# Normalised rows of a four-layer graph network: VectorE's scalar-tensor-tensor form with a repeated second tensor instead of the tensor-scalar form

## The chip, the core and the metric

The kernel runs on one core of a Trainium2 chip. The metric is the device time of one execution in microseconds (us). Three runs of the kernel before took 2252.54, 2250.71 and 2248.42 us, so the median is 2250.71 us.

## What is computed

128 boards of 64 squares, each square a row of 256 values, go through four layers. Each layer normalises its input row by row, applies relu, computes a graph network of the result and adds that to its input:

```
def _layernorm(x, axis=-1, eps=1e-05):
    m = jnp.mean(x, axis=axis, keepdims=True)
    v = jnp.var(x, axis=axis, keepdims=True)
    return (x - m) / jnp.sqrt(v + eps)

    h = jnp.maximum(_layernorm(x, axis=-1), 0.0)
    x = x + _L0_gnn_ref(h, adj, adj, ...)     # attention, 8 heads, static and adjacency masks
    h = jnp.maximum(_layernorm(x, axis=-1), 0.0)
    x = x + _L1_gnn_ref(h, adj, ...)          # attention, 4 heads, adjacency mask
    h = jnp.maximum(_layernorm(x, axis=-1), 0.0)
    x = x + _L2_gnn_ref(h, adj, ...)          # tanh of masked scores, 4 heads, gated
    h = jnp.maximum(_layernorm(x, axis=-1), 0.0)
    x = x + _L3_gnn_ref(h, adj, ...)          # as L1, other weights
```

The change touches only the line `(x - m) / sqrt(v + eps)`, as it is computed in all four layers.

## The kernel before, in words

**Tiling.** A group is 4 boards, that is 256 tokens, held as two tiles (t = 0, 1) of 128 tokens in the partitions by 256 values along the row. There are 32 groups. Two slots work on two groups at once, each with buffers of its own (X, XN, HT, SMALL, F and others carry a 0 or 1), so a loop round takes two groups through all four layers, and there are 16 rounds. Slot 1 runs about half a round behind slot 0.

**Order.** Each engine's program is a fixed list of steps in which the steps of the two slots are merged by a table (`ORDER`), and the engines meet only at semaphores. An engine works its list strictly in order, so a step that waits holds all later steps of that engine, those of the other slot too.

**One normalisation** (eight in a loop round: four layers in each of two slots; 128 in the program) goes through these steps:

- `bn`: VectorE computes statistics of tile 0 and of tile 1 of X (L931).
- `stats`: VectorE merges them into mean and variance (L938) and adds eps (L941); then GpSimd raises two values per partition to the power -0.5 (L410), which gives the reciprocal deviation RSTD, and tells VectorE.
- `norm`: VectorE writes XN = (X - mean) * RSTD, one instruction for each of the two tiles (L949), each telling TensorE when it is done. This is the step that changes.
- `turn`: TensorE transposes XN into PSUM, four 128x128 pieces: (half 0, tile 0), (half 0, tile 1), (half 1, tile 0), (half 1, tile 1) (L505). The first waits for XN's tile 0, the second for its tile 1. ScalarE applies relu and rounds to fp32r (L763), VectorE takes the remainder (L963), and TensorE multiplies both with the layer's weights (L437).

What else the text speaks of: L989, L1003, L1053, L870, L1090 and L1095 are other VectorE operations. GpSimd, beside L410, does one sum X = X + F of 128x512 values in each group's third layer (L423), and one product per group (L415, `row_terms`). On GpSimd's list, L423 of one slot follows directly behind the L410 of the other slot at the same place of every round. L714 are TensorE's transposes of F for the gate in the third layer, L848 ScalarE's copy of those (`cT`), and the `cT` rows of L870 VectorE's remainder of them.

Of the kernel before, what the change touches and what calls it, by code (L numbers as in the profile page):

```python
# [25 lines left out]
ALU = mybir.AluOpType  # L26
# [3 lines left out]
P = 128  # L30
SQ = 64
D = 256
# [107 lines left out]
def build(nc, x_in, adjq_in, adjt_in, mats_in, cols_in, rows_in, cst_in, out):  # L140
# [8 lines left out]
    with ctx:  # L149
# [3 lines left out]
        def sem(name):  # L153
            return ctx.enter_context(nc.semaphore(name))
# [18 lines left out]
        X, XN, HT, MASKA, MASKO, ADJ8, ADJT8, SMALL = ([] for _ in range(8))  # L173
# [10 lines left out]
        MV = [m[:, 12:16].rearrange("p (t c) -> p t c", t=TT) for m in SMALL]  # L184
        VE = [m[:, 16:18] for m in SMALL]
        RSTD = [m[:, 18:20] for m in SMALL]
# [57 lines left out]
        def tanh_buf(s, t):  # L244
# [10 lines left out]
        S = [{n: sem(f"{n}_{s}") for n in ONCE + TWICE + FOUR + NORM + ATTS + ["x_in", "adj_in", "adjT_in", "stored"]}  # L255
             for s in range(SLOTS)]
# [10 lines left out]
        def norm_count(a, v):  # L267

            return v.four[NORM_OF[a]]
# [596 lines left out]
        def _(dve):  # L866
            tt, ts, stt = nc.vector.tensor_tensor, nc.vector.tensor_scalar, nc.vector.scalar_tensor_tensor
# [75 lines left out]
            def norm(s, a, v, before):  # L943
                if a == 0 and before is not None:

                    dve.wait_ge(S[s]["stored"], before)
                dve.wait_ge(S[s]["rstd"], norm_count(a, v))
                for t in range(TT):
                    ts(XN[s][:, t * D:t * D + D], X[s][:, t * D:t * D + D], MV[s][:, t, 0:1],  # L949
                       RSTD[s][:, t:t + 1], ALU.subtract, ALU.mult).then_inc(S[s]["xn_ready"], 1)  # L950

            def masks(s, v):

# [12 lines left out]
            def att(s, k, a, i, v):  # L966
# [7 lines left out]
                elif k == "stats":  # L974
                    stats(s, a, v)
                elif k == "norm":
                    norm(s, a, v, v.before)
                elif k == "masks":
                    masks(s, v)
# [51 lines left out]
            def l2(s, k, i, v):  # L1031
# [3 lines left out]
                elif k == "stats":  # L1035
                    stats(s, L2, v)
                elif k == "norm":
                    norm(s, L2, v, None)
                elif k == "turn":
                    h_lo(s, i, norm_halves(L2, v))  # L1040
# [99 lines left out]
```

## Time and profile before

| | |
|---|---|
| median of three runs | 2250.71 us |
| the profiled execution, whole | 2248.06 us |
| its span, first to last instruction | 2245.9 us |
| mean granted TensorE clock | 0.967 |
| TensorE busy (matmul) | 2011.9 us, 90% |
| TensorE busy (weight loads) | 1818.6 us, 81% |
| VectorE busy | 1445.6 us, 64% |
| ScalarE busy | 1151.8 us, 51% |
| GpSimd busy | 192.2 us, 9% |

All times of single instructions come from one profiled execution. In its rows PE is TensorE's matmul, PEld its weight load, DVE is VectorE, ACT is ScalarE and POOL is GpSimd. `xn<-x,small` reads: the tile XN written from X and SMALL (SMALL holds mean, variance and RSTD). A busy share says nothing of what waits for what; the timeline and the idle times before instructions do.

### The profile page before, as it was taken

The page shows a single profiled execution, that of the slowest core. Times are in us where ns is not written, and L with a number is a line of the kernel's source. Part 1 is how long each engine was busy: PE and PEld are TensorE (multiplying, and loading weights), DVE is VectorE, ACT ScalarE, POOL GpSimd, SP SyncE. Part 2 cuts the span into 40 slices and gives each one's busy share as a digit, 9 for nine tenths or more (in the row PEclk, how much of TensorE's full clock was granted, in tenths as well). Part 3 has the DMA queues.
Part 4 walks back from the last instruction along what each step waited for, and adds up shares of the span by engine and source line. Part 5 has one row for each costly group of instructions (what it writes and reads, how often), then busy time and mean ns, then how long its engine had stood idle before and what let it go on. Part 6 is the DMA issues. An engine that isn't in the chain of part 4 may idle for free.

```text
span 2245.9 us, 53566 instructions
## 1 busy us (share of the span) xinstructions
PE 2011.9 (90%) x21228; PEld 1818.6 (81%) x21228; DVE 1445.6 (64%) x3769; ACT 1151.8 (51%) x3862; POOL 192.2 (9%) x203
## 2 busy tenths in 40 slices
PE   6699989899898989989899998989989899998997
PEld 5588878788887888878788887888888788887885
DVE  4466667667666667667666666666757666666663
ACT  3355555455455555555455454545455455455552
POOL 0000101100001100100110000100101100000100
PEclk8799999999999999999999999999999999999998
DMA  5000000000000000000000000000000000000000
GB/s 174 1 3 12 12 12 12 11 5 9 12 12 12 11 11 2 11 12 11 12 11 2 12 11 12 11 11 2 11 12 11 11 12 2 12 11 12 11 6 5
DMA packets 40630, 30.66 MB, mean 14 GB/s; under 512 B 15664, under 2 KB 40240, under 8 KB 40432
## 3 DMA queue, kind: packets, MB, share of 16 engines
q1 hardware_dynamic: 40432, 27.48, 4.1%
q8 instruction: 190, 3.11, 0.6%
q14 instruction: 8, 0.07, 0.0%
HBM read 19.08 MB, written 8.39 MB: 12 GB/s over the span
## 4 chain that ended last, share of the span: by engine, by line
PE 62%; issue 18%; DVE 12%; ACT 4%; POOL 4%; DMA 1%; DVEq 0%; SPq 0%; POOLq 0%; ACTq 0%
PE ps L437 57%; PE ps L505 4%; POOL small L410 3%; DVE small L931 2%; DVE xn L949 2%; PE ps L581 2%; ACT probs L788 1%; DVE x L1028 1%; DVE wide L1053 1%; DVE f L1062 1%; POOL x L423 1%; DVE aT L870 1%; ACT f L824 1%; ACT wide L816 1%; DVE small L938 1%
## 5 line engine op out<-in xcount | busy, mean ns | idle before, releaser
L437 PE MATMUL ps<-hT,w_hi 128*128 128x256 f32 x2560 | 511.2, 291 | 55.8 <-issue 47.7
L437 PEld LDWEIGHTS ps<-hT,w_hi 128*128 128x128 f32 x2560 | 420.5, 194 | 73.1 <-issue 50.8
L788 ACT ACTIVATE probs<-probs,small 128x64 f32<-128x64 f32 x1024 | 342.1, 339 | 33.2 <-DVE small L1009 31.4
L437 PE MATMUL ps<-hT,w_lo 128*128 128x256 f32 x1280 | 343.1, 288 | 0.0
L437 PEld LDWEIGHTS ps<-hT,w_lo 128*128 128x128 f32 x1280 | 249.2, 195 | 2.7
L437 PE MATMUL ps<-w_hi,hT 128*128 128x256 f32 (+1 forms) x1024 | 249.1, 312 | 0.0
L410 POOL TENSOR_TENSOR small<-small,consts 128x2 f32<-128x2 f32 x128 | 88.8, 694 | 1776.2 <-DVE small L941 1776.2
L437 PE MATMUL ps<-w_hi,oT 128*128 128x256 f32 x768 | 189.2, 311 | 27.4 <-DVE oT L870 27.4
L437 PE MATMUL ps<-wide,w_hi 128*128 128x256 f32 x1024 | 213.1, 285 | 0.2
L788 ACT ACTIVATION_READ_ACCUMULATOR probs<-probs,small 128x1 f32 x1024 | 196.2, 192 | 0.0
L816 ACT ACTIVATE wide<-ps,c_vec 128x256 fp32r<-128x256 f32 x256 | 107.6, 472 | 148.3 <-PE ps L437 148.3
L437 PEld LDWEIGHTS ps<-w_hi,hT 128*128 128x128 f32 x1024 | 175.4, 188 | 8.4
L1053 DVE SCALAR_TENSOR_TENSOR wide<-ps,c_vec,wide 128x256 fp32r<-128x256 f32 x256 | 109.5, 479 | 103.6 <-ACT wide L816 103.5
L437 PEld LDWEIGHTS ps<-w_hi,oT 128*128 128x128 f32 x768 | 147.5, 211 | 32.5 <-DVE oT L870 32.3
L437 PEld LDWEIGHTS ps<-wide,w_hi 128*128 128x128 f32 x1024 | 163.4, 188 | 3.1 <-DVE wide L870 0.7
L949 DVE TENSOR_SCALAR xn<-x,small 128x256 f32<-128x256 f32 x256 | 123.3, 523 | 62.0 <-POOL small L410 59.7
L437 PE MATMUL ps<-w_hi,cT 128*128 128x256 f32 x768 | 159.3, 290 | 0.3 <-ACT cT L848 0.3
L505 PE MATMUL ps<-consts,xn 128*128 128x128 f32 x512 | 116.3, 324 | 46.1 <-DVE xn L949 42.9
L437 PE MATMUL ps<-w_lo,hT 128*128 128x256 f32 (+1 forms) x512 | 149.9, 310 | 0.0
L763 ACT ACTIVATE hT<-ps 128x256 fp32r<-128x256 f32 x256 | 88.4, 383 | 98.5 <-PE ps L505 97.6
L505 PEld LDWEIGHTS ps<-consts,xn 128*128 128x128 f32 x512 | 62.5, 151 | 86.9 <-DVE xn L949 74.2
L437 PE MATMUL ps<-wide,w_lo 128*128 128x256 f32 x512 | 131.8, 280 | 0.0
(123 smaller groups left out, 4342.5 us busy)
## 6 DMA issues: line engine op xcount, KB each, us to landing
raw_mats<-mats SPq DMA_DIRECT2D x8, 1024.0 KB, 11.9
x<-x SPq DMA_DIRECT2D x32, 256.0 KB, 3.0
out<-xn SPq DMA_DIRECT2D x32, 256.0 KB, 3.0
adj<-adjq SPq DMA_DIRECT2D x64, 16.0 KB, 2.0
adjT<-adjt SPq DMA_DIRECT2D x64, 8.0 KB, 2.1
raw_consts<-board_consts SPq DMA_DIRECT2D x1, 451.5 KB, 3.1
raw_rows<-rows SPq DMA_DIRECT2D x1, 256.0 KB, 4.5
bias_cols<-cols SPq DMA_DIRECT2D x1, 6.0 KB, 3.6
```

What stands on the lines that cost most here:

```text
L410: nc.gpsimd.tensor_tensor(RSTD[s], VE[s], HALF.broadcast_to([P, TT]), ALU.pow).then_inc(sm["rstd"], 1)
L423: nc.gpsimd.tensor_tensor(X[s][:, :], X[s][:, :], F[s][:, 0:512], ALU.add).then_inc(sm["x_ha"], 1)
L437: return nc.tensor.matmul(o, lhsT, rhs, start=start, stop=stop, skip_group_check=True)
L505: last = nc.tensor.transpose(bank(s, H_BANKS[c])[:, t * P:t * P + P], XN[s][:, t * D + c * P:t * D + c * P + P], IDENT)
L581: last = nc.tensor.transpose(bank(s, 1 - i)[:, at:at + P], PR[s][:, j, at:at + P], IDENT)
L763: fn(HT[s][:, 0, c, :], bank(s, H_BANKS[c])[:, 0:TOK], ACT.Relu).then_inc(S[s]["hT_hi"], 1)
L788: last = fn(p, p, ACT.Exp, bias=ROWMAX[s][:, row:row + 1], accum_out=ROWSUM[s][:, row:row + 1])
L816: last = fn(e_view(s, 0, oc, i), e_bank(s, E_BANKS[i], oc), ACT.Identity, bias=CVEC[:, oc, i:i + 1])
L824: fn(tanh_buf(s, i), bank(s, 2 + i), ACT.Tanh).then_inc(sm["tanh"], 1)
L931: nc.vector.bn_stats(STATS[s][:, t, :], X[s][:, t * D:t * D + D]).then_inc(S[s]["bn"], 1)
L949: ts(XN[s][:, t * D:t * D + D], X[s][:, t * D:t * D + D], MV[s][:, t, 0:1], RSTD[s][:, t:t + 1], ALU.subtract, ALU.mult).then_inc(S[s]["xn ...
L1053: stt(e_view(s, 1, oc, i), e_bank(s, E_BANKS[i], oc), CVEC[:, oc, i:i + 1], e_view(s, 0, oc, i).bitcast(F32), ALU.add, ALU.subtract).then_ ...
```

## The change

The two instructions of a `norm` step are no longer the form with two per-partition scalars (`tensor_scalar`) but the fused form with a scalar and two tensors (`scalar_tensor_tensor`): (X - mean) * T, where T is the column RSTD read again for each of the 256 elements of a row, through an access pattern with step 0. Semaphores, waits, buffers, the order of all instructions and the values computed stay as they are. Later lines of the file move down by one.

```diff
@@ -946,8 +946,9 @@
                     dve.wait_ge(S[s]["stored"], before)
                 dve.wait_ge(S[s]["rstd"], norm_count(a, v))
                 for t in range(TT):
-                    ts(XN[s][:, t * D:t * D + D], X[s][:, t * D:t * D + D], MV[s][:, t, 0:1],
-                       RSTD[s][:, t:t + 1], ALU.subtract, ALU.mult).then_inc(S[s]["xn_ready"], 1)
+                    stt(XN[s][:, t * D:t * D + D], X[s][:, t * D:t * D + D], MV[s][:, t, 0:1],
+                        RSTD[s][:, t:t + 1].broadcast_to([P, D]), ALU.subtract, ALU.mult
+                        ).then_inc(S[s]["xn_ready"], 1)
```

`ts` and `stt` are `nc.vector.tensor_scalar` and `nc.vector.scalar_tensor_tensor`; D is 256, P is 128, TT is 2.

## Rows read from the trace of the kernel before

**Rows 1.** The page: busy time of each engine, and TensorE's clock in 40 slices.

```profile
PE 2011.9 (90%) x21228; PEld 1818.6 (81%) x21228; DVE 1445.6 (64%) x3769; ACT 1151.8 (51%) x3862; POOL 192.2 (9%) x203
PEclk8799999999999999999999999999999999999998
```

**Rows 2.** The page: the chain that ended last, by engine.

```profile
PE 62%; issue 18%; DVE 12%; ACT 4%; POOL 4%; DMA 1%; DVEq 0%; SPq 0%; POOLq 0%; ACTq 0%
```

**Rows 3.** Line L949 alone: durations in ns, then who waited for it (us, times).

```profile
L949 DVE TENSOR_SCALAR xn<-x,small x256: 401/410/1356, 52.4 to 2223.5; 128x256 f32<-128x256 f32 x128
...
  PEld ps L505: 74.2, 166
  PE ps L505: 42.9, 59
```

**Rows 4.** Groups of VectorE instructions: busy us, mean ns | idle before.

```profile
L1053 DVE SCALAR_TENSOR_TENSOR wide<-ps,c_vec,wide 128x256 fp32r<-128x256 f32 x256 | 109.5, 479 | 103.6 <-ACT wide L816 103.5
...
L963 DVE SCALAR_TENSOR_TENSOR hT<-ps,hT 128x256 fp32r<-128x256 f32 x256 | 99.4, 419 | 21.4 <-ACT hT L763 21.4
...
L1090 DVE SCALAR_TENSOR_TENSOR f<-xn,f 128x256 f32<-128x256 f32 x64 | 27.2, 425 | 2.2
...
L1095 DVE SCALAR_TENSOR_TENSOR x<-f,x 128x512 f32<-128x512 f32 x32 | 22.2, 693 | 3.4
...
L876 DVE TENSOR_SCALAR raw_rows<-raw_rows,raw_consts 128x1024 f32<-128x1024 f32 x1 | 0.8, 753 | 0.0
```

**Rows 5.** Timeline, a normalisation without company: start us, us, what [idle before <-releaser].

```profile
1166.67 0.69 POOL L410 TENSOR_TENSOR small<-small,consts 128x2 f32<-128x2 f32 x1 [13.26 <-DVE small L941]
...
1167.40 0.74 DVE L949 TENSOR_SCALAR xn<-x,small 128x256 f32<-128x256 f32 x2 [0.81 <-POOL small L410]
...
1167.87 1.23 PE L505 MATMUL ps<-consts,xn 128*128 128x128 f32 x4 [0.47 <-DVE xn L949]
...
1168.70 0.81 ACT L763 ACTIVATE hT<-ps 128x256 fp32r<-128x256 f32 x2 [0.82 <-PE ps L505]
```

**Rows 6.** Timeline, a normalisation that starts beside GpSimd's sum L423.

```profile
1145.24 1.28 POOL L423 TENSOR_TENSOR x<-x,f 128x512 f32<-128x512 f32 x1
1145.31 1.68 DVE L949 TENSOR_SCALAR xn<-x,small 128x256 f32<-128x256 f32 x2 [0.80 <-POOL small L410]
...
1145.48 0.60 PE L714 MATMUL ps<-consts,f 128*128 128x128 f32 x4
...
1146.72 0.87 PE L505 MATMUL ps<-consts,xn 128*128 128x128 f32 x4 [0.64 <-DVE xn L949]
1146.91 0.74 DVE L870 TENSOR_TENSOR cT<-ps,cT 128x256 fp32r<-128x256 f32 x2
1147.04 0.31 PEld L505 LDWEIGHTS ps<-consts,xn 128*128 128x128 f32 x3 [0.18 <-DVE xn L949]
```

**Rows 7.** Timeline, a normalisation where TensorE comes a little late.

```profile
1219.07 0.74 DVE L949 TENSOR_SCALAR xn<-x,small 128x256 f32<-128x256 f32 x2 [0.22 <-POOL small L410]
...
1219.57 0.83 PE L505 MATMUL ps<-consts,xn 128*128 128x128 f32 x4
...
1220.66 0.39 PE L437 MATMUL ps<-hT,w_hi 128*128 128x256 f32 x1 [0.25 <-ACT hT L763]
```

**Rows 8.** Timeline, the place where TensorE in some rounds comes later still.

```profile
1111.15 0.73 DVE L949 TENSOR_SCALAR xn<-x,small 128x256 f32<-128x256 f32 x2
...
1112.22 0.46 PEld L505 LDWEIGHTS ps<-consts,xn 128*128 128x128 f32 x4
```

**Rows 9.** Timeline, GpSimd's product L415 and VectorE's L1053 beside it.

```profile
1173.54 1.92 POOL L415 TENSOR_TENSOR row_terms<-rs,consts 128x1024 fp32r<-128x1024 f32 x1 [6.18 <-DVE rs L1048]
...
1174.79 0.88 DVE L1053 SCALAR_TENSOR_TENSOR wide<-ps,c_vec,wide 128x256 fp32r<-128x256 f32 x2 [1.33 <-ACT wide L816]
```

**Rows 10.** Two loop rounds: us, busy of PE, PEld, DVE, ACT, POOL, clock, DMA.

```profile
744.00:877.10 133.10, 121.75 (x1317) 110.08 (x1316) 88.95 (x235) 70.71 (x240) 11.89 (x13) 0.99 0.04 10
...
1281.70:1418.40 136.70, 124.23 (x1317) 112.92 (x1316) 89.07 (x235) 70.81 (x240) 11.86 (x13) 0.96 0.04 10
```

## The prediction, made before the changed kernel was run

> **What bounds the kernel now.** I read the page's busy table first: TensorE is busy 90% of the span and VectorE 64% [rows 1]. The chain that ended last lies 62% on TensorE and 12% on VectorE [rows 2]. So TensorE's fixed list sets the time, and another engine counts where TensorE stands and waits for it. Next I asked for the changed line alone: 256 instructions, median 410 ns, and TensorE does wait for them, 42.9 us ahead of its matmuls and 74.2 us ahead of its weight loads; the loads overlap matmuls, so the two are not added [rows 3]. The 166 waits of loads for 128 normalisations say that TensorE is often held a second time, by the second tile. The timelines show it. With nothing else running, the pair takes 0.74 us, TensorE has been idle for 0.47 us when its first transpose starts, and its four transposes stretch over 1.23 us [rows 5]; in rows 6, at the higher clock, they take 0.87, against 0.60 us for the four of L714, which wait for nothing. Then ScalarE and TensorE's next product hang on these transposes. VectorE's two instructions are thus on the path, and the end of the second is what counts.
>
> One kind of place is different. In each round, once in each slot, the pair starts 0.07 us behind GpSimd's sum L423 and takes 1.68 us instead of 0.74 [rows 6]. The maximum in rows 3 is the first of such a pair, 1356 ns. It ends at 1145.31 + 1.36 = 1146.67, 0.15 us behind the sum's end at 1146.52: it stood still while the sum ran, and did its reading afterwards. I counted 31 such pairs in the trace (first instruction 1341 to 1356 ns); the other 97 have first instructions of 401 to about 414 ns.
>
> **The change part by part.** Nothing is moved, no wait is added; each of the 256 instructions is exchanged for one of another form. Its price is not in the trace, so I bound it. L1053 is the same form with a per-partition scalar, 256 elements, one tensor in PSUM and one in SBUF: 479 ns. L963 is the form with a constant in place of the per-partition scalar: 419. So that scalar costs 60 ns. L1090 has a constant and both tensors in SBUF: 425 [rows 4]. The new instruction has one per-partition scalar (the mean) and two SBUF tensors: 425 + 60 = 485, or 479 by the nearest row; the bottom is 425 (no cost for the scalar). Upwards nothing in the rows goes past 485 without company; a repeated column as second tensor could be dearer, but the trace has no such row in this form. I take 480.
>
> Pairs run back to back with an overlap: 0.74 us for two of 410 ns, 0.88 us for two of 479 [rows 5, 9]. So a pair alone gets 0.88 - 0.74 = 0.14 us longer (bounds: 0.03 with 425 ns, 0.15 with 485).
>
> For a pair beside the sum I need the part that comes after the sum's end, the reading of 256 elements. Two-tensor form: 693 ns at 512 elements less 425 at 256 is 268 ns per 256. One-tensor form: 753 ns at 1024 elements (one scalar), 410 at 256 (two scalars): (753 + 60 - 410) / 768 = 0.52 ns an element, 134 ns per 256; without the correction for the scalar 114 [rows 3, 4]. So the first of the pair ends 268 - 134 = 0.13 us later (0.15 by the other figure), and the second comes 0.07 us later again, 480 less 410: 0.20 us, if it still waits for the sum. The pair would take 1.88 us.
>
> What of it is hidden? At six of the eight normalisations of a round TensorE is idle for the pair already, so all of the 0.14 or 0.20 us falls on the path. At two (one in each slot, [rows 7]) it arrives 0.09 us behind the first tile, 1219.57 against 1219.48, yet its four transposes take 0.83 us, because the second tile ends only at 1219.81; the next product then waits 0.25 us for ScalarE. The second tile's 0.14 us is on the path there too. At one of the six, in 6 of the 16 rounds, TensorE comes 0.34 us behind the whole pair, at 1112.22 against 1111.88 [rows 8], and the 0.14 us is hidden. The steps queued behind on VectorE slip as well: behind the pair of rows 6 comes L870 `cT`, needed by TensorE's product after the transposes; both slip alike, so it is not counted a second time. Later waits of TensorE start from its own earlier output, so I see nothing that gives the delay back.
>
> The sum: 31 x 0.20 = 6.2 us; 97 - 6 = 91 x 0.14 = 12.7 us; together 18.9 us. The profiled execution took 2248.1 us (span 2245.9 and 2.2 around it), so it would take 2267.0. The median of the runs lies 2.6 us above that execution, hence 2269.6; I say 2269.
>
> The clock is the largest noise on it. A round at granted clock 0.99 takes 133.1 us and one at 0.96 takes 136.7 [rows 10]; both kinds stand in this trace. Short stretches at 1.2 instead of 2.4 GHz make the difference; one stands behind the wait of rows 5, where the four transposes take 1.23 us and not 0.87. Longer waits hardly make them rarer. One more or less costs about 1.7 us, half of 136.7 - 133.1 for two of them. I add nothing, and allow 8 of them, 14 us, either way.
>
> **The rule that decides about the sum.** The row shows that a one-tensor instruction on SBUF data stands still while GpSimd's sum runs [rows 6], and that a two-tensor one with a tensor in PSUM does not: L1053 takes its usual 0.88 us for a pair inside GpSimd's L415 [rows 9]. No row shows a two-tensor instruction with both in SBUF beside GpSimd. The Trainium skill, page "SBUF — State Buffer", section "Who interferes with whom", says that such an instruction contends with a GpSimd one that reads SBUF, since its second input comes through the shared read interface, and that the later of the two blocks fully. By this rule the 31 pairs stay blocked and the sum is the above. Without it the 31 pairs would be freed, which is the second rival. The trace agrees with the rule for the cases it has, and leaves this one open.
>
> **The rivals.**
> *The wait goes* (faster). The old instruction read its one tensor two elements at a time and stood still for it; if the new one can run beside the sum, the pair of rows 6 ends at 1145.31 + 0.88 = 1146.19 instead of 1146.99, 0.80 us sooner. TensorE is free at 1146.08 when L714 is through, so it would gain about 0.75 us. 31 x 0.75 = 23 us gained, 12.7 us lost at the other 91: 10 us faster, 2240 us. For it: L1053 beside L415 is undisturbed, and a repeated column is little to read. Against it: X and the column both lie in SBUF, unlike L1053's PSUM tensor. It decides at once: half of the 31 freed already gives 12.7 + 3.1 - 11.6 = 4 us, no measurable change.
> *The delay is given back* (no change). TensorE's waits later in a round could rest on VectorE or ScalarE work of the other slot that is not itself delayed, and shrink. For it: TensorE has other idle time in each round. Against it: the chain of each such wait starts from TensorE output. With four fifths given back it is 4 us: 2254.
> *The clock falls more often* (slower still). Waits of 0.47 us become 0.61. With one more low stretch in each of the 15 full rounds: 15 x 1.7 = 25 us, 2295.
> *The form is the same on the chip*: excluded nearly, as the rows of VectorE name the operation; if both ran at 410 ns the time would stay at 2251.
>
> **How the numbers follow.** Forecast with the clock's noise 0.70; wait gone 0.13; given back or no cost 0.07; clock worse 0.10. The forecast's own range is 2255 to 2283. To hold 8 in 10 with the rivals I take 2246 to 2288. A measurement of this kernel can tell about 0.2%, 4.5 us, from no change. Faster by more: most of the first rival, 0.12. Within: part of it and the given-back case, 0.08. Slower: the forecast and the clock case, 0.80.
>
> **What would show it.** In the changed kernel's profile L949 should read as SCALAR_TENSOR_TENSOR with a median near 480 ns and a maximum near 1490. Pairs should take 0.88 us, and 1.88 beside L423; TensorE's idle time before L505 should rise from 42.9 us by some 15. If the maximum is 480 and the pair beside L423 takes 0.88, the first rival holds. If the median is well above 485, the repeated column has a price of its own, and the time goes up by 0.2 us per pair and 100 ns, 25 us over 128 pairs. If the durations are as said and the span does not follow, the delay was given back: the idle time before other TensorE lines would have shrunk. The clock case would show as rounds of 136 us and more at 0.96, with L949 as forecast.

## The result and the profile after

| | before | changed |
|---|---|---|
| median (lowest to highest), first comparison | 2251.62 us (2248.42 to 2261.88), 4 runs | 2280.27 us (2271.47 to 2289.32), 4 runs |
| median, repeated on one chip with others | 2252.45 us, 24 runs | 2272.26 us, 7 runs |
| profiled execution, whole / span | 2248.06 / 2245.9 us | 2289.32 / 2287.1 us |
| granted clock over the span | 0.967 | 0.954 |

The ratio to the kernel before is 1.012, 95% interval [1.0068, 1.0171], and 1.0076 [1.0049, 1.0104] when repeated. The change makes the kernel slower, by 17 us in the better measurement and 27 us in the first by these ratios (20 and 29 us by the medians); 2269 us had been forecast. The seven repeated executions and the 24 beside them have the same median granted clock, 0.964, and lie 20 us apart.

The page of the changed kernel, against [rows 1, 2]: VectorE is 21 us busier (1445.6 before), and its share of the chain rose from 12 to 15%. TensorE executes the same 21228 matmuls but is 25 us busier; more of them ran at the low clock, which this execution had for 213 us and that of the kernel before for 152 us.

```profile
PE 2036.5 (89%) x21228; PEld 1838.9 (80%) x21228; DVE 1466.6 (64%) x3769; ACT 1149.4 (50%) x3862; POOL 191.9 (8%) x203
...
PEclk8699999999999999999999999999999999999998
...
PE 58%; issue 18%; DVE 15%; ACT 4%; POOL 4%; DMA 1%; DVEq 0%; SPq 0%; POOLq 0%; ACTq 0%
```

The changed line alone, against [rows 3]: minimum, median and maximum in ns are 470, 480, 1493 and were 401, 410, 1356. TensorE's idle time ahead of the matmuls rose from 42.9 to 55.0 us (some 15 had been forecast, it is 12), ahead of the loads from 74.2 to 99.0.

```profile
L949 DVE SCALAR_TENSOR_TENSOR xn<-x,small x256: 470/480/1493, 55.2 to 2264.6; 128x256 f32<-128x256 f32 x128
...
  PEld ps L505: 99.0, 203
  PE ps L505: 55.0, 74
```

The timeline of the changed kernel at the three places of [rows 6, 5, 7], in this order: first beside GpSimd's sum (pair 1.88 us, was 1.68), then alone (0.88, was 0.74), then where TensorE comes late (0.88, was 0.74; four transposes 0.94, were 0.83).

```profile
1166.39 1.27 POOL L423 TENSOR_TENSOR x<-x,f 128x512 f32<-128x512 f32 x1
1166.46 1.88 DVE L949 SCALAR_TENSOR_TENSOR xn<-x,small 128x256 f32<-128x256 f32 x2 [0.80 <-POOL small L410]
...
1168.00 0.94 PE L505 MATMUL ps<-consts,xn 128*128 128x128 f32 x4 [0.76 <-DVE xn L949]
...
1188.87 0.88 DVE L949 SCALAR_TENSOR_TENSOR xn<-x,small 128x256 f32<-128x256 f32 x2 [0.80 <-POOL small L410]
...
1242.14 0.88 DVE L949 SCALAR_TENSOR_TENSOR xn<-x,small 128x256 f32<-128x256 f32 x2 [0.22 <-POOL small L410]
...
1242.68 0.94 PE L505 MATMUL ps<-consts,xn 128*128 128x128 f32 x4
```

Rounds of the changed kernel, against [rows 10] (columns as there). At clock 0.99 a round takes 134.4 to 135.2 us, and took 133.1 to 133.4; the others go up to 139.7 us, and went up to 136.7.

```profile
761.90:897.10 135.20, 121.81 (x1319) 110.33 (x1318) 90.29 (x235) 70.39 (x240) 11.87 (x13) 0.99 0.04 10
897.10:1031.50 134.40, 121.76 (x1319) 109.86 (x1317) 90.21 (x235) 70.64 (x240) 11.89 (x13) 0.99 0.04 10
...
1439.70:1577.70 138.00, 125.85 (x1319) 113.76 (x1317) 90.27 (x235) 70.61 (x240) 11.83 (x13) 0.95 0.04 10
```

**The delay, place by place.** From the timelines I took the time from the start of each pair to the start of the next, as the median of those among 14 rounds in which no low clock falls into the stretch (for the sixth one round of the kernel before, else five to fourteen):

| from pair | 1 (beside the sum) | 2 | 3 | 4 | 5 (beside the sum) | 6 |
|---|---|---|---|---|---|---|
| before | 8.14 | 13.93 | 9.13 | 33.14 | 8.13 | 13.96 |
| changed | 8.34 | 14.08 | 9.26 | 33.20 | 8.33 | 14.08 |
| difference | 0.20 | 0.15 | 0.13 | 0.06 | 0.20 | 0.12 |

The stretch from pair 7 to pair 8 has the low clock in every round of the kernel before, and TensorE reaches pair 8 early in some rounds and late in others [rows 8], so the last two have no clean figure.

### The profile page after: what moved, and what is told of

Read it like the earlier page. It is cut to its first block, busy times and chain, and to the rows that moved or that the text cites. A ratio compares the mean times of both kernels' runs of the same rounds, so it can differ in the third digit from the quotient of the medians.

```text
span 2287.1 us, 53566 instructions
## 1 busy us (share of the span) xinstructions
PE 2036.5 (89%) x21228; PEld 1838.9 (80%) x21228; DVE 1466.6 (64%) x3769; ACT 1149.4 (50%) x3862; POOL 191.9 (8%) x203
## 4 chain that ended last, share of the span: by engine, by line
PE 58%; issue 18%; DVE 15%; ACT 4%; POOL 4%; DMA 1%; DVEq 0%; SPq 0%; POOLq 0%; ACTq 0%
PE ps L437 54%; DVE xn L949 3%; POOL small L410 3%; PE ps L505 2%; DVE small L931 2%; PE ps L581 2%; ACT probs L788 1%; DVE x L1029 1%; DVE small L938 1%; DVE f L1063 1%; ACT wide L816 1%; POOL x L423 1%; DVE aT L870 1%; ACT f L824 1%; DVE wide L1054 1%
## 5 line engine op out<-in xcount | busy, mean ns | idle before, releaser
L437 PE MATMUL ps<-hT,w_hi 128*128 128x256 f32 x2560 | 527.8, 298 | 54.0 <-issue 45.9
L437 PEld LDWEIGHTS ps<-hT,w_hi 128*128 128x128 f32 x2560 | 435.2, 201 | 71.5 <-issue 49.2
L437 PE MATMUL ps<-hT,w_lo 128*128 128x256 f32 x1280 | 352.1, 294 | 0.0
L437 PEld LDWEIGHTS ps<-hT,w_lo 128*128 128x128 f32 x1280 | 258.3, 202 | 2.7
L949 DVE SCALAR_TENSOR_TENSOR xn<-x,small 128x256 f32<-128x256 f32 x256 | 143.6, 601 | 61.4 <-POOL small L410 59.5
```

The source lines that it names most:

```text
L437: return nc.tensor.matmul(o, lhsT, rhs, start=start, stop=stop, skip_group_check=True)
L949: stt(XN[s][:, t * D:t * D + D], X[s][:, t * D:t * D + D], MV[s][:, t, 0:1], RSTD[s][:, t:t + 1].broadcast_to([P, D]), ALU.subtract, ALU.m ...
```

## The experiments

**The changed kernel again.** No edit.

> The changed kernel once more, beside the others on one chip. Theory A (each pair of L949 ends later, TensorE waits for it, and low stretches of its clock come on top): 16 to 32 us over before. Rival B (the first measurement stood high because of the clock alone, the direct cost is hidden): within 8 us of before. The direct part is 31 x 0.20 + 91 x 0.14 = 19 us.

2272.26 us, ratio 1.0076 [1.0049, 1.0104], 17 us. Durations of L949 were 470/480/1493 again. Rival B falls. The first measurement's extra 10 us is not in the instructions. The granted clock is on record for each of these executions: the four of the first comparison had 0.954, 0.960, 0.961 and 0.965, the seven of this one 0.964 in the median, and the 24 of the kernel before beside them 0.964 too. The profiled executions are not typical of either: the first has the lowest clock of its four, and this one (0.960) is the slowest of its seven, while that of the kernel before (0.967) is faster than most. Summed from the trace's record of the clock, rounds 2 to 15 of this profile hold 6.8 us at 1.2 GHz each, those of the first profile 9.0, and those of before 5.8.

**What the form costs.** Each layer got a form of its own (`a == 2` is the fourth layer here, the last branch the third):

```diff
+                    if a == 0:
+                        last = stt(xn, x, mean, rstd.broadcast_to([P, D]), ALU.subtract, ALU.mult)
+                    elif a == 1:
+                        last = stt(xn, x, mean, X[s][:, (1 - t) * D:(1 - t) * D + D], ALU.subtract, ALU.mult)
+                    elif a == 2:
+                        last = stt(xn, x, 0.0, rstd.broadcast_to([P, D]), ALU.subtract, ALU.mult)
+                    else:
+                        last = ts(xn, x, 0.0, rstd, ALU.subtract, ALU.mult)
```

> One look for durations: each layer's L949 pair in a form of its own, so layers 2 to 4 compute other values than the reference. First layer: as changed. Second: the second tensor is the other tile of X, read element by element, in place of the repeated column. Fourth: constant 0 in place of the mean. Third: the old form with constant 0 in place of the mean. Without the sum beside it, theory (two tensors go one element at a time, a per-partition scalar costs 60 ns, the repeated column nothing): 480, 480, 420 and 350 ns. Rival (the repeated column has a price of its own): the second is clearly below the first. The time itself: between before and after, about 2260 us.

The answer for the tile XN on VectorE, durations as minimum/median/maximum in ns (one of the forms also stands beside the sum, hence its 1492):

```profile
L951 DVE SCALAR_TENSOR_TENSOR xn<-x,small x64: 473/479/485, 52.6 to 2137.8; 128x256 f32<-128x256 f32 x64
L953 DVE SCALAR_TENSOR_TENSOR xn<-x,small x64: 470/482/1492, 79.0 to 2172.1; 128x256 f32<-128x256 f32 x64
L957 DVE TENSOR_SCALAR xn<-x,small x64: 344/350/354, 101.6 to 2193.2; 128x256 f32<-128x256 f32 x64
...
L955 DVE SCALAR_TENSOR_TENSOR xn<-x,small x64: 416/422/427, 152.4 to 2240.7; 128x256 f32<-128x256 f32 x64
```

The single execution took 2265.30 us, where about 2260 had been expected. 479 with the repeated column and 482 with a full second tensor: the column costs nothing of its own. Without the scalar it is 422, and the old form with one scalar instead of two takes 350 and not 410: a per-partition scalar costs 57 to 60 ns in both forms. So the change drops one scalar (60 ns) and adds a second tensor (422 - 350 + 60 = about 130 ns), 70 ns in sum.

**Does the new form wait for GpSimd, and why?** In both kernels GpSimd's sum was replaced by a memset of 128x1024, which only writes:

```diff
-                    nc.gpsimd.tensor_tensor(X[s][:, :], X[s][:, :], F[s][:, 0:512], ALU.add).then_inc(sm["x_ha"], 1)
+                    alone(pool)
+                    nc.gpsimd.memset(WIDE[s][:, 0, 0, :].bitcast(F32), 0.0).then_inc(sm["x_ha"], 1)
```

> The kernel before with GpSimd's sum (two reads, one write) replaced by a memset of 128x1024 in a tile that is out of use: GpSimd then only writes, some 0.95 us by the memset of L395. X + F is left out of the result. By the rule of the Trainium skill (a one-tensor instruction that runs two elements at a time takes the read and the write interface it shares with GpSimd): the 31 pairs still wait, their first instructions end 0.15 us behind the memset, about 1.0 us long. Rival (only GpSimd's reads block): they take 410 ns.

> The changed kernel with the same memset in place of the sum; X + F is left out of the result. By the rule of the Trainium skill (a two-tensor instruction takes only the read interface, so it contends only with a GpSimd instruction that reads): all L949 at 480 ns, the 31 beside the memset too. Rival (any GpSimd access to its memory blocks it): about 1.1 us at the 31 places.

Timeline with the old form (the pair starts 0.09 us behind the memset and takes 1.32 us):

```profile
1153.07 0.95 POOL L424 MEMSET wide<- 128x1024 f32 x1
1153.16 1.32 DVE L950 TENSOR_SCALAR xn<-x,small 128x256 f32<-128x256 f32 x2 [0.80 <-POOL small L410]
```

And with the new form, at the same place of the program (0.88 us, as if alone):

```profile
1163.18 0.95 POOL L424 MEMSET wide<- 128x1024 f32 x1
1163.27 0.88 DVE L950 SCALAR_TENSOR_TENSOR xn<-x,small 128x256 f32<-128x256 f32 x2 [0.80 <-POOL small L410]
```

The old form's maximum over the run is 1008 ns, the new form's 487. So the two forms wait for GpSimd for different reasons. The one-tensor form stands still even for a GpSimd instruction that only writes; the two-tensor form does not, yet it does for the sum, which reads (1.88 us above). The Trainium skill, page "SBUF — State Buffer", section "Who interferes with whom", says that a VectorE instruction in a 2-port mode, which `tensor_scalar` can enter, contends with GpSimd, and that one with two SBUF inputs contends only with a GpSimd instruction that reads SBUF. The two runs agree with it in either half, if the one-tensor form ran in such a mode, which the trace does not name. The 1.88 us beside the sum are what put the first rival out. The times, 2269.11 and 2279.46 us, are single runs of kernels that leave out work.

**Time alone, without the new form.** The old form, with a small instruction between the two:

```diff
                     ts(XN[s][:, t * D:t * D + D], X[s][:, t * D:t * D + D], MV[s][:, t, 0:1],
                        RSTD[s][:, t:t + 1], ALU.subtract, ALU.mult).then_inc(S[s]["xn_ready"], 1)
+                    if t == 0:
+                        tt(SPARE[s], IDENT[:, 0:30], IDENT[:, 0:30], ALU.add)
```

> The kernel before with the old form, and one small VectorE instruction on spare values (128x30, two tensors) between the two of each pair. By L1017 and L1019 it takes some 0.18 us, 0.10 behind the overlap, so each pair is 0.10 us longer and the second tile as much later. Theory A (only the time of the pair counts, not its form): 122 x 0.10 = 12 us over before, plus or minus the clock. Rival C (the delay of the pair is given back, and the changed kernel is slow for another effect of its form, as on GpSimd or on other VectorE work): within 4 us of before.

2268.49 us, ratio 1.0067 [1.0041, 1.0094], 15 us (12 expected), on a pair that is 0.10 us longer (0.84 us):

```profile
1187.87 0.41 DVE L950 TENSOR_SCALAR xn<-x,small 128x256 f32<-128x256 f32 x1 [0.81 <-POOL small L411]
1188.20 0.18 DVE L953 TENSOR_TENSOR small<-consts 128x30 f32<-128x30 f32 x1
1188.30 0.41 DVE L950 TENSOR_SCALAR xn<-x,small 128x256 f32<-128x256 f32 x1
```

Here the first tile is ready as early as before, and only the second is late: its end is what counts. Rival C falls.

**The sum out of the way.** One wait added on GpSimd, to each form:

```diff
                     pool.wait_ge(sm["ha_sb"], v.once)
+                    pool.wait_ge(sm["hat_lo"], v.two[0])
```

> The kernel before with one wait added on GpSimd: its sum X = X + F (L423) starts only when the remainder of the gate's first half (VectorE's L870 cT, queued behind the pair of L949) is done. The pair then runs without the sum beside it. Theory A (the 31 long pairs are the sum's doing): no L949 over 430 ns, pairs 0.74 us everywhere, TensorE's idle time of 0.64 and 0.55 us before L505 nearly gone at 31 places, so 31 x 0.6 = 19 us less than before, 2232 us. Rival (the pair of that place is long for another reason, or TensorE then waits for cT or the sum instead): durations unchanged, or changed with no gain, within 5 us of before.

> The changed kernel with the same added wait on GpSimd's sum. Theory A: L949 at 480 ns everywhere, pairs 0.88 us, the direct cost against the kernel with the late sum and the old form is 122 x 0.14 = 17 us, and it stands 31 x 0.75 = 23 us below the changed kernel: about 2251, the time of the kernel before. Rival (what was lost at the 31 places was not the waiting for the sum): it stays within 8 us of the changed kernel.

The pairs did as forecast; in the kernel with the old form the sum starts behind them and TensorE does not wait ahead of its first transpose:

```profile
748.38 0.74 DVE L950 TENSOR_SCALAR xn<-x,small 128x256 f32<-128x256 f32 x2 [0.80 <-POOL small L410]
...
748.98 0.74 PE L506 MATMUL ps<-consts,xn 128*128 128x128 f32 x4
...
749.88 1.29 POOL L424 TENSOR_TENSOR x<-x,f 128x512 f32<-128x512 f32 x1 [1.54 <-DVE cT L871]
```

From pair 1 to pair 2 it now takes 7.34 us instead of 8.14, with either form, and from pair 5 to pair 6 7.43 us with either. So with the sum out of the way the 0.14 us of these two pairs no longer reach TensorE's list at all. But the time did not follow the gain: 2256.99 us, ratio 1.0007 [0.9987, 1.0027] with the old form, and 2274.19 us, 1.0084 [1.0054, 1.0115] with the new one, where I expected 0.991 and 1.000. The rounds say where it went (columns as before, clock third from the right):

```profile
883.30:1018.40 135.10, 124.56 (x1319) 113.72 (x1318) 87.20 (x236) 70.55 (x240) 11.94 (x12) 0.95 0.04 10
1018.40:1153.00 134.60, 124.50 (x1318) 113.13 (x1317) 87.11 (x236) 70.40 (x240) 11.95 (x12) 0.96 0.04 10
1153.00:1286.00 133.00, 122.72 (x1319) 111.38 (x1318) 87.13 (x236) 70.67 (x240) 11.95 (x12) 0.97 0.04 10
```

A round holds 12.0 us at 1.2 GHz (13.4 with the new form), twice the 5.8 of the kernel before. It is so outside the profiles too: the twelve executions with the old form had granted clocks of 0.943 to 0.952, the kernel before 0.960 to 0.969. The gain at the pairs was eaten by TensorE's clock. A fit over 14 rounds of each of the 13 profiles, with one level for each kernel and one common price, gives 0.35 us lost for each us at the low clock (a round scatters 0.25 us about it), and these levels at no low clock: before 132.3, changed 133.5 (133.5 again when repeated), late sum 130.8 with the old form and 131.7 with the new, small instruction 133.1 us. The change is thus 1.2 us a round, and late sum with the old form -1.5. The common price is a simplification: rounds with the least low time (3.4 us) differ by 1.7 us between before and changed, those with 10.2 us by only 0.4.

**Filling TensorE's waits.** To see whether these low stretches come from TensorE's waits that stand close together, transposes of the identity into banks out of use were put ahead of three of them:

```diff
+            def filler(o, n):
+                for _ in range(n):
+                    nc.tensor.transpose(o[:, 0:P], IDENT, IDENT)
...
+                if a == L2 and c == 0:
+                    filler(bank(s, H_BANKS[0]), 3)
...
+                    if a == 2 and i == 1:
+                        filler(bank(s, 2), 7)
...
+                    if a == 2:
+                        filler(bank(s, 2), 3)
```

> The kernel before with thirteen transposes of the identity into unused PSUM banks, for each of the 32 groups, put ahead of three waits of TensorE that stand close together: seven ahead of the second half of the last layer's probabilities (idle 1.10 us), three ahead of that layer's product with v (0.53 us), three ahead of the third layer's normalised rows (0.46 us). They fill idle time that is there anyway. Theory D (the low stretches of the clock come from these close waits): the time at 1.2 GHz falls from 5.8 us a round to under 3, and at 0.35 us lost for each us at the low clock the time falls by 15 to 25 us, to about 2232. Rival (the low stretches come from elsewhere, such as the 3.7 us wait at the loop's end, or the fillers delay work): the low time stays, and the time is the same or up to 10 us more.

> The same fillers, and GpSimd's sum started late as in late_sum_old_form. By the rounds of that kernel, corrected for its time at the low clock, the late sum is worth 1.5 us a round, 23 us, and was eaten by 12 us of low clock a round instead of 6. Theory D: with the fillers the low time is under 5 us a round, and the time is 25 to 40 us below before, about 2220. Rival: low time near 12 us a round again and the time within 8 us of before.

> The changed kernel with the thirteen fillers for each group. With the low clock held to 3 to 7 us a round, the direct cost should stand alone over filled_waits (2248.7): 31 x 0.20 + 91 to 97 x 0.14 = 19 to 20 us, so 2268, ratio to before 1.006 to 1.008. Rival (half of the first 27 us over before was a cost of the form that the sum does not have): 2275 or more.

> The changed kernel with the fillers and the late sum: no pair beside the sum. Direct cost over filled_waits_late_sum (2214.1): 122 to 128 x 0.14 = 17 to 18 us, so 2232. Rival (the 0.14 us is partly given back where TensorE has other waits): under 2224.

| | old form: us, ratio to before | new form: us, ratio to before |
|---|---|---|
| fillers | 2248.69, 0.9979 [0.9966, 0.9992] | 2261.20, 1.0026 [1.0014, 1.0038] |
| fillers and late sum | 2214.07, 0.9823 [0.9798, 0.9847] | 2230.20, 0.9885 [0.9868, 0.9902] |

The fillers alone gave 5 us where 15 to 25 were expected; they lowered the low time only to 4.6 us a round and cost 0.5 us a round themselves by the fit. With the late sum they lowered it from 12.0 to 4.1 us, and the time fell to 39 us below the kernel before (25 to 40 expected). In all four kernels with fillers no low clock falls between pair 1 and pair 7 in any of the 14 rounds; with the late sum and the old form alone every round had some there. What is left stands between pairs 7 and 8. One window of 1800 us shows the clock, first the late sum without fillers:

```profile
350.00:2150.00 1800.00, 1661.68 (x17534) 1513.24 (x17535) 1165.46 (x3127) 943.07 (x3218) 158.64 (x159) 0.96 0.04 10
```

and with them, where in the same 1800 us TensorE gets through 754 more matmuls (some 350 of them fillers, at 26 a round):

```profile
350.00:2150.00 1800.00, 1692.60 (x18288) 1539.03 (x18287) 1185.62 (x3186) 957.59 (x3284) 162.03 (x163) 0.99 0.04 10
```

Between the columns stands the price of the form with a steadier clock: 0.9885 - 0.9823 is 0.62%, 14 us (16.1 by the medians, 17 to 18 expected), and 0.47%, 11 us, with the sum beside it (12.5 by the medians, 19 to 20 expected). By their intervals these prices are good to about 7 and 4 us. In both profiles with the new form the pairs take 0.88 us, and 1.88 where the sum stands beside them, so the instructions are as forecast. Up to the seventh pair of a round the new form with fillers is later by about 1.0 us; over the whole round, rounds with one low stretch take 133.9 us with the old form and 134.8 with the new: 0.9. The last two pairs thus add nothing there, where I had counted 0.14 us for each, less the hidden ones.

**The price at equal clock.** The medians above still mix the form with the clock: the new form with fillers had a granted clock of 0.9725 in the median, the old one 0.970. As the clock of all executions but three of the first comparison is on record, executions with the same clock can be compared (mean us, number of executions). The time at 1.2 GHz, half the full clock, is twice the missing share of the clock, times the span:

| kernels | clock | old form | new form | difference |
|---|---|---|---|---|
| as they are | 0.964 | 2254.0 (17) | 2272.2 (3) | 18 |
| as they are | 0.966 | 2249.7 (7) | 2270.1 (1) | 20 |
| with fillers | 0.971 | 2247.5 (2) | 2264.4 (3) | 17 |
| with fillers | 0.972 | 2245.8 (2) | 2262.5 (3) | 17 |
| late sum | 0.947 | 2257.2 (3) | 2268.7 (2) | 11 |

A fit over 134 executions of the nine kernels that ran more than once, with one level for each kernel and one common price, gives the same: 0.39 us lost for each us at 1.2 GHz, and the new form costs 18.2 us (95% interval 17.4 to 19.0) in the program as it is, 16.5 with fillers, 11.8 with the late sum and 12.6 with both; the small instruction costs 11.6 (12 expected). By the same fit the late sum is worth 27 us with the old form (an extrapolation, since no execution without it had so low a clock), and 24 with fillers in (25 at the one clock that both have, 0.972), where 19 had been expected of it. The late-sum prices are low in part for the reason seen above: pairs 1 and 5 cost nothing there, 31 x 0.14 = 4 us of the 17 to 18. The 39 us of fillers and late sum together are 24 from the late sum, less 6 that the fillers cost, and 22 from the low clock, which these executions had for 106 us in the median and the kernel before for 162.

## Why the prediction was right, point by point

- **The price of the instruction** (taken 480 ns, bounds 425 and 485): 480, by the duration; that it is a scalar at 60 ns and a second tensor, and that the column is free, was shown by the four forms.
- **The pair** (0.14 us longer; 0.20 beside the sum, to 1.88 us): 0.14 and 0.20, in the profile. The maximum forecast at 1490 ns is 1493.
- **The wait for the sum stays**: right, and shown for its reason by the memset pair of runs.
- **The path**: TensorE's list slips by about the whole delay at pairs 1, 2, 3, 5 and 6. At pair 4 only 0.06 us arrives. The six stretches of the table add up to 0.86 us a round, 13 us over 15.5 rounds; 18.2 us at equal clock leaves about 0.3 us a round for pairs 7 and 8 together, an estimate, which is their 0.14 us each. With fillers in, nothing could be measured behind pairs 7 and 8, and with the late sum nothing arrives from pairs 1 and 5. So my sentence "I see nothing that gives the delay back" was wrong at pair 4, and wrong for the variants of the program. What gives the delay back at these places I did not test. (Pair 8 comes before TensorE in five rounds of the profile and not in six, which is 0.1 us.)
- **The sum** of 18.9 us: 18.2 us at equal clock in the program as it is, and 1.2 us a round (19 us) by the fit over rounds. So the sum was right by its terms and not by luck. It was too high for the kernels with the late sum, where I had expected 17 to 18 and measured 12 to 13.
- **The clock** (nothing added, 14 us either way): right for the repeated median, where both kernels had 0.964. The first median, 2280, lies 11 us above the forecast, with clocks of 0.960 and 0.961 in the middle of its four executions; at 0.39 us for each us at 1.2 GHz the step from 0.964 is 6 us of that. The price of a low stretch was mis-sized: I had 1.7 us (and half of 136.7 - 133.1 is 1.8), but the two rounds differ by two stretches of 3.4 us each, and at 0.35 to 0.39 us per us one costs 1.2 to 1.3. Whether the longer waits bring more low time is not shown: all eleven executions of the changed kernel have a median clock of 0.964, as before. Taking waits away did bring more.

## What to carry to other kernels

Price an exchange of VectorE forms by the number of per-partition scalars and by whether one or two tensors are read, each from rows of the kernel's own trace, and charge it where TensorE waits for the last instruction of the group. The cheap case is one tensor in SBUF: with one scalar it took 350 ns here, while L986 of the kernel before, the same form with one scalar and its tensor in PSUM, takes 480, as much as two tensors. Look for GpSimd work that starts just ahead of it: which forms stand still depends on whether GpSimd reads. And when a wait is removed and the time does not move, compare the granted clock, and executions with the same clock, before blaming the path: here a gain of 1.5 to 1.7 us a round was there all along, and thirteen idle transposes for each group let it through by holding the clock up (2214 us, 1.8% under the kernel before, the best of all versions tried, with the old form).

## What the runs showed of the hardware that I had not expected

- Taking 0.8 us of waiting away twice a round doubled the time at 1.2 GHz, from 5.8 to 12.0 us a round; why the clock answers so is open.
- The effects do not add: late sum alone 1.0007, fillers alone 0.9979, both 0.9823.
- The kernels with the late sum and new form, and with the memset and new form, ran nearly every round at 136.3 to 136.7 us, and the kernel before had rows of rounds at 133.1. The former hold 13.7 us at 1.2 GHz each, the latter 3.4, so rounds repeat their low stretches for a while. No run here says why.
